# Rope stage of a decoder layer regrouped from pairs of heads to fours, with the rope weights as 32x64 tiles

## The chip, the cores and the metric

The kernel runs on one core of a Trainium2 chip. The metric is the device time of one execution in microseconds. Three runs before the change gave a median of 886.24 us (886.09 to 887.56).

## What is computed

One decoder layer over 32 sequences of 64 tokens, width 256, all in float32. Three blocks follow one another, each with a residual and a layer norm: linear attention, cross attention with rotary positions, and a mixture of 32 experts with the best 8. The change lies in the cross attention, and in what is computed between its parts. Cut to that (16 heads, R = 64, D_C = 64, D_CQ = 192, K = 128):

```python
q_hk = (hidden_q @ Wq.T).reshape(Bv, Sv, H, K)
q_big = jnp.einsum('bshk,hkq->bshq', q_hk, w_kc_q)
q_big = _apply_rope(q_big, sin_q[None, :, None, :], cos_q[None, :, None, :])
kv_r = _apply_rope(kv_c, sin_k[None], cos_k[None])
q_r = jnp.einsum('bshq,hqr->bhsr', q_big, W_qr)
k_r = jnp.einsum('bld,hdr->bhlr', kv_r, W_kr)
scores = jnp.einsum('bhsr,bhlr->bhsl', q_r, k_r)
attn = jax.nn.softmax(scores, axis=-1)
```

Rope multiplies each of the 192 rows of `q_big` by a cosine and adds its partner row, 96 rows away, times a sine.

## The kernel before

The tokens go in four blocks of 512. For each block a linear attention part, then `pairs` (the rope stage) and then `cross` (scores, softmax, context) run. The five engines have a program of their own each, written out by hand and joined by semaphores. `cross(b)` also holds the linear attention of block b + 1, so the order is `linear(0)`, `pairs(0)`, then `cross(b)` and `pairs(b + 1)` for b = 0 to 2, then `cross(3)` and the experts. Weights are folded once: `fold_a` multiplies Wq by w_kc_q for each head (`a_hi`, `a_lo`), `fold_m` multiplies W_qr by W_kr (`m_w`, 64 columns a head), so that a head's query goes straight to the 64 channels of the latent keys.

The rope stage handles 8 pairs of heads. For a pair, TensorE (PE) makes three chunks of 128 rows into three PSUM banks: 18 matmuls of 128x128 by 512 columns (`split_matmuls`, L245 to L247: a float32 product as three products of high and low parts). Chunk 0 has rows 0 to 63 of both heads, chunk 1 their partners 96 to 159, chunk 2 rows 64 to 95 and 160 to 191. VectorE (DVE) multiplies from PSUM with the tables `ropeq` (`times`, L1055): four products of chunks 0 and 1 into `prod`, two of chunk 2 straight into `roped`. GpSimd (POOL) adds the two pairs of products (L749). Chunk 2 is not added: its rows go into the next product twice, once with the cosine and once with the sine. `latent_q` (L1436) then multiplies four chunks of `roped` with `m_w`: 16 matmuls of 64x64 by 256 columns, each of which the profile shows as two records, so 32. They use the four quarters of the array, and stand on PE behind the 18 products of the following pair. ScalarE (ACT) copies the result to `lq` (L842).

PE waits at pair p for the DVE products of pair p - 2 (`s_rp`); two sets of three banks alternate. Banks 6 and 7 hold the result of `latent_q`, which waits for the ACT copy of the pair before (`s_lq`). Between the rope products DVE also runs, for the block before, the norm of its last 128 tokens (`norm2`, behind pair 0) and its expert routing (`shift_logits` behind pair 2, six parts of `route` behind pairs 3 to 5), and for the next block the root mean square norm (`rms`, behind pair 5). Within each of these, a small instruction waits for the one before it.

At the end of the stage PE runs `latent_q(6)` and `latent_q(7)`, turns the next block's x (`turn_x`), computes `scores(0)`, and DVE starts the softmax (`shift`, L1100) while PE runs projections.

## Time and profile before

| | |
|---|---|
| median of 3 runs | 886.24 us |
| the profiled execution | 886.25 us, of which the span is 884.4 |
| PE busy | 851.1 us |
| DVE busy | 634.8 us |
| ACT, POOL busy | 277.7, 144.9 us |
| granted clock of PE | 0.995 of full speed |
| rope stage of block 0 | from 53.3 us |
| rope stages of blocks 1 to 3 | from 159.9, 268.5 and 377.6 us |
| experts | from 460.8 us |

Busy time is the time in which at least one instruction of the engine runs. Matmuls overlap, so the spacing of their starts tells more than their duration. Line numbers are those of the kernel.

### The profile page before, as it was taken

To read this page: it belongs to the slowest core of one execution; us is meant where nothing else is said; L and a number is where in the kernel's file an instruction comes from. 1 tells how busy PE (TensorE), PEld (TensorE's weight loads), DVE (VectorE), ACT (ScalarE), POOL (GpSimd) and SP (SyncE) were. 2 spreads that over 40 slices of the span, in tenths; PEclk is the share of its full clock that TensorE was granted. 3 is DMA by queue.
4 is the path that set the end of the run, shared out by engine and by line. 5 is a ranking of instruction groups with operands and counts; after the bars stand their busy time and mean duration, and the time that the engine had idled before them with its cause. 6 is when DMAs were issued, how large, how long until landed. Compare 5 with 4: busy or idle time off the path is not lost.

```text
span 884.4 us, 14757 instructions
## 1 busy us (share of the span) xinstructions
PE 851.1 (96%) x5742; PEld 671.2 (76%) x5742; DVE 634.8 (72%) x1383; ACT 277.7 (31%) x498; POOL 144.9 (16%) x123
## 2 busy tenths in 40 slices
PE   8999999999999989999899999999999999999995
PEld 6967677676777767777578778888888888887884
DVE  5566787878878888788677776766575666666587
ACT  4431243112422124220353522433323333232242
POOL 2024301333013330133340400300000000000120
PEclk9999999999999999999999999999999999999998
DMA  9210000100001000000230014110212020000011
GB/s 345 115 37 1 1 2 1 49 1 18 1 1 49 1 17 1 0 25 4 81 109 1 25 32 150 44 59 1 90 48 66 0 85 29 35 1 1 1 47 49
DMA packets 12830, 35.84 MB, mean 41 GB/s; under 512 B 1504, under 2 KB 2400, under 8 KB 12256
## 3 DMA queue, kind: packets, MB, share of 16 engines
q1 hardware_dynamic: 12768, 34.98, 11.5%
q8 instruction: 42, 0.69, 0.4%
q14 instruction: 20, 0.16, 0.1%
HBM read 30.33 MB, written 2.36 MB: 37 GB/s over the span
## 4 chain that ended last, share of the span: by engine, by line
PE 85%; DVE 9%; issue 3%; ACT 2%; DMA 0%; POOL 0%; ACTq 0%; DVEq 0%
PE ps L245 21%; PE ps L246 20%; PE ps L247 20%; PE ps L1436 7%; PE ps L1516 5%; PE ps L1507 3%; PE ps L1308 2%; PE ps L1492 1%; PE ps L1345 1%; PE ps L1483 1%; DVE xT_lo L968 1%; PE ps L1375 1%; PE ps L1301 1%; PE ps L1291 1%; PE ps L1262 1%
## 5 line engine op out<-in xcount | busy, mean ns | idle before, releaser
L518 DVE TENSOR_TENSOR su<-sg,ps 128x512 f32<-128x512 f32 x96 | 66.0, 687 | 121.4 <-PE ps L247 118.2
L245 PE MATMUL ps<-y_hi,f_hi 128*128 128x512 f32 x384 | 151.2, 394 | 1.3 <-issue 1.3
L247 PE MATMUL ps<-y_hi,f_lo 128*128 128x512 f32 x384 | 149.5, 389 | 0.0
L246 PE MATMUL ps<-y_lo,f_hi 128*128 128x512 f32 x384 | 149.4, 389 | 0.0
L376 ACT ACTIVATE sg<-ps 128x512 f32<-128x512 f32 x96 | 57.4, 599 | 250.6 <-PE ps L247 250.6
L749 POOL TENSOR_TENSOR roped<-prod 128x512 f32<-128x512 f32 x64 | 80.9, 1286 | 169.9 <-DVE prod L1055 169.9
L1055 DVE TENSOR_TENSOR prod<-ps,ropeq 128x512 f32<-128x512 f32 x128 | 79.3, 681 | 27.2 <-PE ps L247 27.0
L245 PEld LDWEIGHTS ps<-y_hi,f_hi 128*128 128x128 f32 x384 | 72.1, 188 | 16.9 <-issue 2.2
L247 PEld LDWEIGHTS ps<-y_hi,f_lo 128*128 128x128 f32 x384 | 72.1, 188 | 15.2
L246 PEld LDWEIGHTS ps<-y_lo,f_hi 128*128 128x128 f32 x384 | 72.1, 188 | 15.1 <-issue 0.5
L245 PE MATMUL ps<-xT_hi,a_hi 128*128 128x512 f32 x192 | 78.4, 408 | 3.7 <-DVE xT_lo L968 3.7
L245 PE MATMUL ps<-h_hi,f_hi 128*128 128x512 f32 x192 | 75.4, 393 | 1.4 <-DVE h_lo L349 1.4
L524 DVE TENSOR_TENSOR hc<-su,cb 128x512 f32<-128x512 f32 x96 | 72.0, 750 | 6.0
L246 PE MATMUL ps<-xT_lo,a_hi 128*128 128x512 f32 x192 | 75.4, 393 | 0.0
L247 PE MATMUL ps<-xT_hi,a_lo 128*128 128x512 f32 x192 | 74.9, 390 | 0.0
L247 PE MATMUL ps<-h_hi,f_lo 128*128 128x512 f32 x192 | 74.8, 389 | 0.0
L246 PE MATMUL ps<-h_lo,f_hi 128*128 128x512 f32 x192 | 74.8, 389 | 0.0
L842 ACT ACTIVATE lq<-ps 128x512 f32<-128x512 f32 x28 | 16.8, 599 | 159.0 <-PE ps L1436 159.0
L1436 PE MATMUL ps<-roped,m_w 64*64 64x256 f32 x1024 | 63.1, 383 | 2.9 <-ACT lq L842 2.9
L349 DVE TENSOR_TENSOR h_lo<-hc,h_hi 128x512 fp32r<-128x512 f32 x88 | 62.6, 712 | 0.1
L370 ACT ACTIVATE h_hi<-hc 128x512 fp32r<-128x512 f32 x96 | 59.9, 624 | 3.4 <-DVE hc L524 3.4
L1516 PE MATMUL ps<-u_w,roped 128*128 128x256 f32 x256 | 58.2, 380 | 2.1 <-ACT roped L874 2.1
(161 smaller groups left out, 1336.9 us busy)
## 6 DMA issues: line engine op xcount, KB each, us to landing
cb<-routing SPq DMA_DIRECT2D x32, 256.0 KB
f_raw<-in_L_ffn_gate_up_proj SPq DMA_DIRECT2D x8, 768.0 KB, 6.2
f_raw<-in_L_ffn_down_proj SPq DMA_DIRECT2D x8, 384.0 KB, 7.0
xb<-in_x SPq DMA_DIRECT2D x4, 512.0 KB, 4.2
lq<-in_L_xattn_Wq SPq DMA_DIRECT2D x1, 2048.0 KB, 14.7
x2T_all<-in_L_xattn_Wo SPq DMA_DIRECT2D x1, 2048.0 KB, 12.0
x2T_all<-x2T SPq DMA_DIRECT2D x4, 512.0 KB, 3.3
roped<-in_L_xattn_w_kc_q SPq DMA_DIRECT2D x1, 1536.0 KB, 10.0
```

What stands on the lines that cost most here:

```text
L245: pe.matmul(dst, l_hi, r_hi, start=first, stop=False, skip_group_check=check)
L246: pe.matmul(dst, l_hi, r_lo, start=False, stop=False, skip_group_check=check)
L247: return pe.matmul(dst, l_lo, r_hi, start=False, stop=last, skip_group_check=check)
L349: eng.tensor_tensor(h_lo[:, k % 3], hc[:, k % 2], h_hi[:, k % 3].bitcast(F32), ALU.subtract).then_inc(s_hlo, 1)
L370: act.activation(h_hi[:, k % 3], hc[:, k % 2], ACT.Copy).then_inc(s_hhi, 1)
L376: act.activation(sg[:, k % 2], bank(2 * (k % 2)), ACT.Silu).then_inc(s_sg, 1)
L518: dve.tensor_tensor(su[:, k % 2], sg[:, k % 2], bank(2 * (k % 2) + 1), ALU.mult).then_inc(s_su, 1)
L524: dve.tensor_tensor(hc[:, k % 2], su[:, k % 2], cb[:, w, cols(n)], ALU.mult).then_inc(s_hc, 1)
L749: pool.tensor_tensor(roped[:, p % 2, k], prod[:, 2 * k], prod[:, 2 * k + 1], ALU.add)\
L1055: return dve.tensor_tensor(t64(dst), t64(bank(src)), ropeq[:, table, :].unsqueeze(1).broadcast_to((P, SEQS, SEQ)), ALU.mult)
L1436: mm = pe.matmul(ps[r:r + 64, q_bank(p, h), 0:256], m_w[i, p, k * DC:(k + 1) * DC], roped[i, p % 2, k, 256 * th:256 * th + 256], start=k = ...
L1516: mm = pe.matmul(ps[:, f, 0:D], ct[:, c, :], u_w[:, (c + 4 * (t // 2)) % 8, :], start=c == 0, stop=c == PAIRS - 1)
```

## The change

The rope stage works on four heads (a quad: pairs 2g and 2g + 1, j = 0 or 1) and makes six chunks for them, each with 32 rows of each head. Chunks 0 and 1, 2 and 3, 4 and 5 are partners. A step for two partner chunks is called a slot; 12 slots make a block, with 12 matmuls of 512 columns each. Slots use banks 0, 1 and 2, 3 in turn; PE waits at slot t for the DVE products of slot t - 2. DVE makes four products a slot into three buffers in turn (`made`), POOL adds both pairs, and a ring of four slots holds the sums. No row goes into `latent_q` twice. `latent_q(g, c)` has 16 matmuls of 32x64 by 256 columns for each slot, on the eight 32x64 parts of the array; each of the four row parts writes to a bank of its own (banks 4 to 7). The three of a quad stand together, behind slots 4, 7 and 10; those of the last quad behind slot 11, with `turn_x` and the scores of six pairs moved ahead of the last one.

On DVE the norm, the routing and the root mean square norm are cut into single steps. After each product `side` issues the steps due there: `norm2` in slots 0 and 1, `shift_logits` behind slot 3, 22 routing steps from the third product of slot 4 to the end of slot 9, 12 steps of the root mean square norm in slots 6 to 8. The arithmetic of these steps is as before. ACT has its other work (`x1` copy, squares, exp) ahead of its `lq` copies. `fold_m` writes 32 columns at a time, in 24 matmuls for two pairs in place of 16. The order and tables of the inputs follow the new rows. Left out below: `route_step` and `rms_step` with the old instructions one by one, and the host's reordering.

```diff
+QUADS = PAIRS // 2
+SLOTS = 3 * QUADS
...
-    a_hi = sb(att, "a_hi", [P, KC, PAIRS, 3 * P], F32R)
-    a_lo = sb(att, "a_lo", [P, KC, PAIRS, 3 * P], F32R)
-    m_w = sb(att, "m_w", [P, PAIRS, 4 * DC])
-    ropeq = sb(att, "ropeq", [P, 6, SEQ])
+    a_hi = sb(att, "a_hi", [P, KC, QUADS, 6 * P], F32R)
+    a_lo = sb(att, "a_lo", [P, KC, QUADS, 6 * P], F32R)
+    m_w = sb(att, "m_w", [P, QUADS, 6 * DC])
+    ropeq = sb(att, "ropeq", [P, 12, SEQ])
...
-    roped = sb(att, "roped", [P, 2, 4, BT])
+    roped = sb(att, "roped", [P, 8, BT])
...
+    prod2 = sb(att, "prod2", [P, 2, BT])
...
-    LOGITS = ps[:, 5, 0:TILES * EXPERTS]
+    LOGITS = ps[:, 7, 0:TILES * EXPERTS]
     m_bank = lambda g, h: 4 + (g + h) % 2
-    q_bank = lambda p, h: (6 if p < PAIRS - 1 else 2, 7)[h]
+    lq_bank = lambda b, g, j: 0 if g == QUADS - 1 and j == 1 and b < BLOCKS - 1 else 4 + 2 * j
+    score_bank = lambda b: 2 if b < BLOCKS - 1 else 0
+    turn_bank = lambda b: 2 - score_bank(b)
+    made = lambda i: (prod[:, 0:2], prod[:, 2:4], prod2[:, 0:2])[i % 3]
+    a_pair = lambda a, k: a[:, k % KC, k // KC // 2].rearrange("p (r h j c) -> p r h j c", h=2, j=2, c=32)[:, :, :, k // KC % 2]
+    a_psum = lambda k: ps[:, k % 4, 0:384].rearrange("p (r h c) -> p r h c", h=2, c=32)
...
-    C_BANKS = (6, 7, 5, 4)
+    C_BANKS = (2, 3, 6, 4)
...
-            for p in range(PAIRS):
+            for t in range(SLOTS):
                 for k in range(2):
-                    pool.wait_ge(s_rp, 24 * b + 3 * p + k + 1)
-                    if p >= 2 and k == 0:
-                        pool.wait_ge(s_qr, 8 * b + p - 1)
-                    pool.tensor_tensor(roped[:, p % 2, k], prod[:, 2 * k], prod[:, 2 * k + 1], ALU.add)\
+                    pool.wait_ge(s_rp, 24 * b + 2 * t + k + 1)
+                    if t >= 4 and k == 0:
+                        pool.wait_ge(s_qr, SLOTS * b + t - 3)
+                    pool.tensor_tensor(roped[:, 2 * (t % 4) + k], made(2 * t + k)[:, 0], made(2 * t + k)[:, 1], ALU.add)\
                         .then_inc(s_rope, 1)
...
+        def lq_out(b, p):
+            f = lq_bank(b, p // 2, p % 2)
+            act.wait_ge(s_qr, SLOTS * b + 3 * (p // 2) + 3)
+            act.activation(lq[:, p].rearrange("p (h n) -> p h n", h=2), ps[:, f:f + 2, 0:256], ACT.Copy)\
+                .then_inc(s_lq, 1)
+
         def pairs(b, later, following):
             act.wait_ge(s_x1, 4 * b + 4)
             if later:
                 x2T_out(b - 1, 2, 5)
-            else:
-                act.activation(x1[:], xn[:], ACT.Copy).then_inc(s_x1c, 1)
-            for p in range(PAIRS):
-                act.wait_ge(s_qr, 8 * b + p + 1)
-                if p < PAIRS - 1:
-                    act.activation(lq[:, p].rearrange("p (h n) -> p h n", h=2), ps[:, 6:8, 0:256], ACT.Copy)\
-                        .then_inc(s_lq, 1)
-                else:
-                    act.activation(lq[:, p, 0:256], ps[:, q_bank(p, 0), 0:256], ACT.Copy)
-                    act.activation(lq[:, p, 256:512], ps[:, q_bank(p, 1), 0:256], ACT.Copy).then_inc(s_lq, 1)
-                if later and p == 0:
-                    x2T_out(b - 1, 3, 2)
-                    act.activation(x1[:], xn[:], ACT.Copy).then_inc(s_x1c, 1)
-                if later and p == 2:
-                    act.wait_ge(s_lsub, b)
-                    act.activation(rt[:, 1], rt[:, 0], ACT.Exp).then_inc(s_lexp, 1)
-                if following and p == 1:
-                    act.wait_ge(s_x1c, b + 1)
-                    squares(b + 1)
+                x2T_out(b - 1, 3, 4)
+            act.activation(x1[:], xn[:], ACT.Copy).then_inc(s_x1c, 1)
+            if following:
+                act.wait_ge(s_x1c, b + 1)
+                squares(b + 1)
+            if later:
+                act.wait_ge(s_lsub, b)
+                act.activation(rt[:, 1], rt[:, 0], ACT.Exp).then_inc(s_lexp, 1)
+            for p in range(PAIRS - 2):
+                lq_out(b, p)
+            for m in range(2 if following else 0):
+                xT_hi_out(b + 1, m, s_xt, s_xthi)
+            lq_out(b, PAIRS - 2)
+            lq_out(b, PAIRS - 1)
...
+            def side(i):
+
+                if later and i + 1 < len(NORM2_PARTS):
+                    for j in range(NORM2_PARTS[i], NORM2_PARTS[i + 1]):
+                        norm2_step(b - 1, 3, j)
+                if later and i == 4 * 3 + 3:
+                    shift_logits(b - 1, LOGITS)
+                if later and 0 <= i - (4 * 4 + 2) < ROUTE_COUNT:
+                    route_step(b - 1, i - (4 * 4 + 2))
+                if following and 0 <= i - 4 * 6 < RMS_STEPS:
+                    rms_step(b + 1, i - 4 * 6)
+
             own.need()
-            for p in range(PAIRS):
-                if following and p == 6:
-                    rms(b + 1)
-                f = 3 * (p % 2)
-                for k in range(3):
-                    if k < 2:
-                        if p >= 1:
-                            dve.wait_ge(s_rope, 16 * b + 2 * p - 1 + k)
-                        dve.wait_ge(s_q, 24 * b + 3 * p + 2)
-                        times(prod[:, 2 * k], f + k, 2 * k)
-                        times(prod[:, 2 * k + 1], f + 1 - k, 2 * k + 1).then_inc(s_rp, 1)
-                    else:
-                        if p >= 2:
-                            dve.wait_ge(s_qr, 8 * b + p - 1)
-                        dve.wait_ge(s_q, 24 * b + 3 * p + 3)
-                        times(roped[:, p % 2, 2], f + 2, 4)
-                        times(roped[:, p % 2, 3], f + 2, 5).then_inc(s_rp, 1)
-                if later and p == 0:
-                    norm2(b - 1, 3)
-                if later and p == 2:
-                    shift_logits(b - 1, LOGITS)
-                if later and 3 <= p < 6:
-                    route(b - 1, 2 * p - 6)
-                    route(b - 1, 2 * p - 5)
+            for t in range(SLOTS):
+                f, table = 2 * (t % 2), 4 * (t % 3)
+                for k in range(2):
+                    if 2 * t + k >= 3:
+                        dve.wait_ge(s_rope, 24 * b + 2 * t + k - 2)
+                    dve.wait_ge(s_q, 24 * b + 2 * t + 2)
+                    times(made(2 * t + k)[:, 0], f + k, table + 2 * k)
+                    side(4 * t + 2 * k)
+                    times(made(2 * t + k)[:, 1], f + 1 - k, table + 2 * k + 1).then_inc(s_rp, 1)
+                    side(4 * t + 2 * k + 1)
...
+        NORM2_PARTS, RMS_STEPS, ROUTE_COUNT = (0, 1, 2, 4, 6, 8, 10, 11), 12, 22
...
-                for p in (2 * g, 2 * g + 1):
-                    for k in range(4):
+                for c in range(6):
+                    for j in range(2):
                         for h in range(2):
                             r = slice(64 * h, 64 * h + 64)
-                            o = (p % 2 * 4 + k) * DC
-                            mm = pe.matmul(ps[r, m_bank(g, h), o:o + DC], l_qr[r, p, k, :], r_kr[r, p, :],
+                            q = 64 * h + 32 * j
+                            mm = pe.matmul(ps[q:q + 32, m_bank(g, h), c * DC:(c + 1) * DC],
+                                           l_qr[r, 2 * g + j, 32 * c:32 * c + 32], r_kr[r, 2 * g + j, :],
...
+            def latent_q(g, c):
+
+                for k in range(2):
+                    pe.wait_ge(s_rope, 24 * b + 2 * (3 * g + c) + k + 1)
+                    w = slice((2 * c + k) * DC, (2 * c + k + 1) * DC)
+                    ring = 2 * ((3 * g + c) % 4) + k
+                    for th in range(2):
+                        for j in range(2):
+                            for h in range(2):
+                                i = slice(64 * h + 32 * j, 64 * h + 32 * j + 32)
+                                r = 64 * (h ^ th)
+                                mm = pe.matmul(ps[r:r + 64, lq_bank(b, g, j) + h, 0:256], m_w[i, g, w],
+                                               roped[i, ring, 256 * th:256 * th + 256],
+                                               start=c + k == 0, stop=c + k == 3)
+                mm.then_inc(s_qr, 1)
...
+            for t in range(SLOTS):
+                g, c = t // 3, t % 3
+                if t == 1:
                     pe.wait_ge(s_bdT, 2 * b + 2)
+                if t >= 2:
+                    pe.wait_ge(s_rp, 24 * b + 2 * t - 2)
+                for k in range(2):
+                    a = slice((2 * c + k) * P, (2 * c + k + 1) * P)
+                    for kc in range(KC):
+                        mm = split_matmuls(pe, bank(2 * (t % 2) + k), a_hi[:, kc, g, a], a_lo[:, kc, g, a],
+                                           xT_hi[:, kc, :], xT_lo[:, kc, :], kc == 0, kc == KC - 1)
+                    mm.then_inc(s_q, 1)
+                if later and t == 0:
                     pe.wait_ge(s_bdT, 2 * b + 2)
                     turn_x2(b - 1, 2, 5)
+                if later and t == 2:
                     pe.wait_ge(s_r2, 4 * b)
                     pe.wait_ge(s_ct, 8 * b)
+                    turn_x2(b - 1, 3, 4)
+                if later and t == 3:
                     logits(b - 1, LOGITS)
+                if t in (4, 7, 10):
+                    g = t // 3 - 1
+                    if g >= 1:
+                        pe.wait_ge(s_lq, 8 * b + 2 * g)
+                    if later and g == 0:
                         pe.wait_ge(s_lsub, b)
+                    for c in range(3):
+                        latent_q(g, c)
+            pe.wait_ge(s_lq, 8 * b + PAIRS - 2)
+            pe.wait_ge(s_rp, 24 * b + 22)
+            latent_q(QUADS - 1, 0)
+            latent_q(QUADS - 1, 1)
+            for m in range(2 if following else 0):
+                turn_x(n, m, s_xn, s_xt)
+            if following:
+                pe.wait_ge(s_rp, 24 * b + 24)
+            scores(b, 0, 0, PAIRS - 2)
+            latent_q(QUADS - 1, 2)
...
-                pe.wait_ge(s_lq, 8 * b + 7)
-                turn_x(n, 0, s_xn, s_xt)
-                pe.wait_ge(s_lq, 8 * b + 8)
-                turn_x(n, 1, s_xn, s_xt)
-                scores(0)
                 projection(n, 0)
+                scores(b, 0, PAIRS - 2)
                 projection(n, 1)
-                scores(1)
+                scores(b, 1)
...
-                pe.wait_ge(s_lq, 8 * b + 7)
+                pe.wait_ge(s_rp, 24 * b + 24)
                 turn_c(pe, 0)
-                pe.wait_ge(s_lq, 8 * b + 8)
                 turn_c(pe, 1)
-                pe.wait_ge(s_rp, 24 * b + 24)
+                scores(b, 0, PAIRS - 2)
                 turn_c(pe, 2)
-                scores(0)
-                keep_warm(6, 3)
-                scores(1)
+                keep_warm(6, 7)
+                pe.wait_ge(s_cT, 2)
+                scores(b, 1)
```

## Rows read from the trace of the kernel before

**Rows 1.** The page's chain that ended last, by engine, share of the span.

```profile
PE 85%; DVE 9%; issue 3%; ACT 2%; DMA 0%; POOL 0%; ACTq 0%; DVEq 0%
```

**Rows 2.** Busy time by stretch, rope stage of block 1: stretch, length, PE, PEld, DVE, ACT, POOL.

```profile
159.86:207.70 47.84, 47.84 (x356) 35.37 (x356) 41.29 (x123) 7.09 (x19) 17.74 (x14) 1.00 0.09 30
```

**Rows 3.** Groups of instructions in 159.7 to 208 us: count, busy us, mean ns.

```profile
L1055 DVE TENSOR_TENSOR prod<-ps,ropeq 128x512 f32<-128x512 f32 x30 | 18.6, 681 | 3.0 <-PE ps L247 3.0
L749 POOL TENSOR_TENSOR roped<-prod 128x512 f32<-128x512 f32 x14 | 17.7, 1290 | 35.4 <-DVE prod L1055 35.4
```

**Rows 4.** Timeline of one pair, block 0: start us, length us, then the instruction.

```profile
67.96 1.96 PE L1436 MATMUL ps<-roped,m_w 64*64 64x256 f32 x32
69.84 0.50 PE L245 MATMUL ps<-xT_hi,a_hi 128*128 128x512 f32 x1
70.19 0.40 PE L246 MATMUL ps<-xT_lo,a_hi 128*128 128x512 f32 x1
...
72.51 0.39 PE L247 MATMUL ps<-xT_hi,a_lo 128*128 128x512 f32 x1
...
73.01 0.69 DVE L1055 TENSOR_TENSOR prod<-ps,ropeq 128x512 f32<-128x512 f32 x1 [2.56 <-PE ps L247]
...
73.87 0.39 PE L247 MATMUL ps<-xT_hi,a_lo 128*128 128x512 f32 x1
74.19 0.45 PE L1436 MATMUL ps<-roped,m_w 64*64 64x256 f32 x4
```

**Rows 5.** L1436 in stretches of 0.02 us; in brackets the records running.

```profile
67.96:67.98 0.02, 0.02 (x4) 0.02 (x4) 1.00 0.00 0
...
68.44:68.46 0.02, 0.02 (x7) 0.02 (x3) 1.00 0.00 0
```

**Rows 6.** The chain in order of time: start us, length us, what.

```profile
17.09 2.08 PE ps L1331 x64
...
117.86 1.09 PE ps L1483 x64
...
121.45 3.46 PE ps L1516 x16
```

**Rows 7.** Timeline of DVE in block 1, routing steps and products.

```profile
186.57 0.47 DVE L1157 MAX8 top<-rt 128x8 f32<-128x32 f32 x4
187.08 0.09 DVE L1160 MATCH_VALUE_LOAD rt<-top,rt 128x8 f32 x1
...
187.25 0.08 DVE L1160 MATCH_VALUE_LOAD rt<-top,rt 128x8 f32 x1
...
187.85 0.29 DVE L1162 SCALAR_TENSOR_TENSOR rt<-rt 128x128 f32<-128x128 f32 x1
188.06 2.48 DVE L1055 TENSOR_TENSOR prod<-ps,ropeq 128x512 f32<-128x512 f32 x4
...
192.09 0.17 DVE L1169 TENSOR_SCALAR rs<-rs 128x4 f32<-128x4 f32 x1
192.17 0.22 DVE L1170 SCALAR_TENSOR_TENSOR rs<-top,rs 128x4 f32<-128x4 f32 x1
```

**Rows 8.** Timeline, end of block 1's rope stage, PE and DVE.

```profile
207.48 0.39 PE L247 MATMUL ps<-xT_hi,a_lo 128*128 128x512 f32 x1
...
210.47 2.20 PE L1436 MATMUL ps<-roped,m_w 64*64 64x256 f32 x32 [0.72 <-ACT lq L842]
...
215.38 0.68 DVE L1100 TENSOR_REDUCE small<-ps 128x8 f32<-128x512 f32 x1
```

**Rows 9.** Timeline, end of block 3's rope stage, PE and DVE.

```profile
425.32 0.39 PE L247 MATMUL ps<-xT_hi,a_lo 128*128 128x512 f32 x1
...
433.28 0.69 DVE L1100 TENSOR_REDUCE small<-ps 128x8 f32<-128x512 f32 x1 [5.15 <-issue]
```

**Rows 10.** Timeline behind `fold_m`, weight load of PE's next product.

```profile
19.10 0.19 PEld L245 LDWEIGHTS ps<-xT_hi,w_hi 128*128 128x128 f32 x1
```

**Rows 11.** Timeline of DVE at the start of block 1's rope stage, last of `norm2`.

```profile
162.51 0.41 DVE L954 TENSOR_SCALAR x<-x,small 128x256 f32<-128x256 f32 x1
```

227 lines of the change are left out of this document (116 added, 111 removed).

## The prediction, made before the changed kernel ran

> **What bounds the kernel now.** I read the chain that ended last first: 85% of it is PE [rows 1]. Then the stretches: in the rope stage of block 1 PE is busy all of its 47.84 us, but DVE is busy 41.29 of them [rows 2], and of its idle time 3.0 us is a wait for PE's products [rows 3]. So this stage is PE's, with DVE close behind. The timeline of a pair gives its period: `latent_q` starts at 67.96 and again at 74.19, 6.23 us later [rows 4]. Inside, from the second to the eighteenth product (70.19 to 73.87) there are 16 spacings of 0.230 us [rows 4]; the first takes 0.35 (69.84 to 70.19), 0.12 more, as every start behind another kind of work does. 18 x 0.230 = 4.14, which leaves 2.09 us of a pair for `latent_q`. Its 32 records start in sets of four: four run at 67.96, and seven or eight near each new start [rows 5]. A full-array product with 256 columns takes 3.46 / 16 = 0.216 us a record [rows 6]. Eight sets at 0.216 are 1.73 us; the other 0.36 us of the 2.09 is the price of going from full-array work to tiles and back.
>
> **What the change removes on PE.** The products with `a_hi` and `a_lo` stay 144 a block. `latent_q` had 8 x 32 = 256 records a block and gets 12 x 32 = 384, but if eight tiles run at once there are 48 sets in place of 64. No row before shows eight tiles at once. The lower bound of a set is the stream of one tile, 0.216 us, which a full array and four tiles share. The upper bound is two sets of four behind each other, 0.432. Between them: 64 records of 64 columns take 2.08 us where two tiles work (L1331) and 1.09 where four do (L1483) [rows 6], so a set of two takes 0.065 and a set of four 0.068; twice the tiles cost 0.003 us a set, and one record went out every 0.017 us, 0.136 for eight, under 0.216. I take 0.216.
>
> The Trainium skill, "TensorEngine Tiling (Array Packing)", Key Properties, says that different tiles run loads and matmuls in parallel and lists 32x64 as eight tiles; the trace bears this out for four 64x64 tiles and shows nothing on eight. By it the sum stays as it is. "TensorE: Matmul & The Clock Gate", Part 3, gives about 4 ns for each further tile of a set; the four tiles here show no such surplus per set (four tiles and the full array both take 0.216), and as an estimate from that page four more tiles on 192 sets would take back 3 us.
>
> Before the last product of a block stood six bursts of 2.09, 12.5 us. Now three stand there, of 12 sets each: 3 x (2.59 + 0.36) = 8.9. That is 3.7 us less a block, 14.7 in four, if nothing waits.
>
> **What waits instead.** The slots are the new point. PE takes 12 x 0.230 = 2.76 us for one, and slot t may not start before DVE has finished slot t - 2, because two pairs of banks alternate. DVE starts 0.27 us behind the last of the products (72.51 + 0.23 to 73.01) [rows 4], its products start every 0.60 (four in 2.48 with a last one of 0.68), and the last ends 0.69 on: 0.27 + 1.80 + 0.69 = 2.76. With 0.05 for the signal (my estimate) it is 2.81 against 2.76, and PE's restart costs 0.12. So wherever two slots follow each other with no burst between, PE loses 0.16, before any small step. Before, a set of three banks had 6.23 us between its reuses against some 3.8 of DVE, and this could not happen.
>
> The small steps that now stand between two products of a slot lengthen it. Their price, when the product hides their latency, is the start spacing: 0.21 for a 128x128 step (187.85 to 188.06), 0.08 for a tiny one (192.09 to 192.17), 0.66 for four match-and-replace (four times 187.08 to 187.25), 0.42 for four MAX8 [rows 7]. Below, they could cost nothing; above, their price was the spacing with the wait for each other, some 1.4 times that (0.77 us from 187.08 to 187.85, 0.51 from 186.57 to 187.08). By place:
>
> - Slots 2, 4, 7 and 10 of block 0 have only the 0.16 each, and slot 10 0.27 more from three tiny steps: 0.9 us.
> - Start of blocks 1 to 3: the turn of x2 now stands behind slot 0, 2.76 us into the stage, and wants `norm2(2)`, which ended at 162.92, 3.06 us in [rows 11]: 0.35. Then the `norm2(3)` steps in slots 0 and 1 (some 0.6 and 0.8 us) make slots 2 and 3 wait 0.25 and 0.5. Together 1.1.
> - Slot 7: slot 5 has the routing steps with MAX8 and match-and-replace between its products: 0.21 + 0.42 + 0.66 = 1.29, so 0.16 + 1.29 = 1.45.
> - Slot 10: slot 8 has three tiny steps (0.27) and three routing steps (0.7): 0.16 + 0.97 = 1.13, without the tiny ones 0.86 in block 3.
> - The turns and the logits no longer stand beside a burst, so two restarts of 0.12 come in: 0.2.
>
> Sum of the waits: 0.9 in block 0, 3.9 in blocks 1 and 2, 3.6 in block 3. Against 3.7: +2.8, -0.2, -0.2, +0.1, so 2.5 us faster in all. In the later blocks the waits take the whole gain of the tiles.
>
> POOL has 24 additions of some 1.27 us a block for 16 [rows 3], 31 us of 48, one for each 1.2 us of products in a slot; it lags up to 1.4 us behind DVE. `latent_q` runs a slot and more later, so this is hidden; without that cover it would cost up to 1.4 us a burst. The ring of four slots is free in time, since the burst behind slot 4 frees slot 0 before POOL reaches slot 4.
>
> **Behind the last product.** In block 1 the softmax starts on DVE 7.67 us after it (207.71 to 215.38) [rows 8]; 0.72 of that was `latent_q(7)` waiting for the ACT copy, which goes. Two bursts (4.2) become one of two slots and one of a single slot, 2.1 + 1.2 = 3.3. But `projection(n, 0)`, 6 x 0.230 + 0.12 = 1.5, now stands before the scores of the last pairs: 7.67 - 0.72 - 0.9 + 1.5 = 7.55. 0.1 for each of three blocks. From there to the first turn of weights DVE's own chain decides, unchanged. PE then has one projection and not two to cover the softmax's start; that wait falls where PE would have waited anyway. In block 3 (7.73 before [rows 9]) no projection comes in, but the last `latent_q` waits for POOL's last sum, 0.27 + 1.80 + 0.69 + 0.07 + 1.29 = 4.1 behind the last product; then 0.5 for it, 1.2 for two ACT copies and 0.6 for the scores, with 0.3 of handshakes: 6.7. Of the 1.0 I take 0.7, because ACT now has the third `cT` copy ahead of the exponentials. Together 1.0.
>
> **The folds.** `fold_m` writes with four 64x32 tiles at once and not two 64x64: 48 records for 64, in sets of four at 0.068. Its second half takes 0.8 for 2.08 [rows 6], and the next product stood at its end, 19.10 [rows 10]. Bounds 0 and 2.5; DVE's copies of `m_w` come between, so I take 0.6. `fold_a` has the same records and copies of the same size in another order: nothing. The first load is smaller and is not waited for. `route` in the experts part has the same steps: nothing.
>
> **Sum.** 2.5 + 1.0 + 0.6 = 4.1. The profiled execution took 886.25, the median 886.24, so I forecast 882.1.
>
> **Rivals.**
>
> - Eight tiles do not run at once. From a set of 0.216 + 4.1 / 192 = 0.237 on the change no longer gains; at 0.432 it costs 192 x 0.216 = 41 us, less some 4 us of DVE waits that this hides: 919. For it: nothing in the trace has more than four at once, and four banks are written at a time for two. Against: two to four tiles cost 0.003. A set between 0.237 and 0.3 gives 886 to 898. Chance 0.08 for the full price, 0.10 for between.
> - DVE is not late. If small steps vanish behind products, the waits fall to 0.9 or less a block and the sum is 4 x 2.8 + 1.6 = 12.8: 873; without handshakes at all 870. For it: DVE's busy time sees its chains shortened. Against: 41.29 of 47.84 busy. Chance 0.17.
> - DVE is later than I think. At 1.4 times the step price blocks 1 to 3 lose 1.5 us more each: 887, no change or slightly slower. Chance 0.12.
> - The forecast, 878 to 886, around 882.1: 0.53.
>
> The range 868 to 891 takes in the second, third and last and the lower part of the first: 0.8 of the chance or a little more. A measurement here tells about 0.2% (1.8 us) from no change. Faster: 0.40 of the 0.53 and the 0.17, 0.59 with a little of the rest. Within 0.2%: 0.16. Slower: 0.25.
>
> **What would show it.** In the profile after: `latent_q` bursts of about 2.6 us for 96 records, with eight records starting within 0.05 us and sets 0.216 apart (if they are 0.43, the first rival). PE's waits for DVE's products before slots 7 and 10, near 1.4 and 1.1 us in blocks 1 to 3, under 0.5 in block 0. Block 0's rope stage near 43 us from first to last product for 45.7, the others' near 48. The prediction is wrong if block 1's stage is much shorter than 47 us (DVE was not late) or the bursts are longer than 3.1 us.

## The result, and the profile of the changed kernel

The changed kernel takes 906.6 us (median of 4 runs, 905.4 to 909.3), the kernel before 886.26 beside it (4 runs, 886.09 to 887.56): a ratio of 1.0234, 95% interval 1.0221 to 1.0246. It is 20.3 us slower; forecast were 882.1 us, in a range of 868 to 891. The profiled execution took 905.4 us, its span is 903.6.

First the stages, by the starts of the products with `a_hi` and `a_lo` (the end is the start of a block's last product plus 0.23; by these starts the stages of blocks 2 and 3 of the kernel before begin at 268.8 and 377.7 us). A crossing is the stretch from the end of one block's rope stage to the start of the next one's.

| stretch | before, us | after, us | difference | forecast |
|---|---|---|---|---|
| up to block 0's rope stage | 53.30 | 57.78 | +4.5 | -0.6 |
| rope stage of block 0 | 45.74 | 43.61 | -2.1 | -2.8 |
| of block 1 | 47.85 | 54.86 | +7.0 | +0.2 |
| of block 2 | 47.85 | 56.21 | +8.4 | +0.2 |
| of block 3 | 47.85 | 50.82 | +3.0 | -0.1 |
| three crossings (60.82, 61.08, 61.06 before) | 182.96 | 181.45 | -1.5 | -0.3 |
| behind block 3's last product | 458.9 | 458.9 | 0.0 | -0.7 |

The sum of the differences is the 19.2 us between the spans. So the loss has two places: the start, and the rope stages of blocks 1 to 3.

The timeline of TensorE (PE) in block 1 of the changed kernel, start us, length us, and in brackets its idle time and what ended it; the first burst of latents is with it:

```profile
165.09 0.41 PE L1425 MATMUL ps<-ident,x 128*128 128x128 f32 x2 [0.15 <-DVE x L960]
173.56 0.41 PE L1425 MATMUL ps<-ident,x 128*128 128x128 f32 x2 [2.26 <-DVE x L1149]
...
181.59 2.85 PE L1509 MATMUL ps<-roped,m_w 32*64 32x256 f32 x96
...
191.25 0.50 PE L254 MATMUL ps<-xT_hi,a_hi 128*128 128x512 f32 x1 [1.14 <-DVE prod L1058]
...
202.35 0.50 PE L254 MATMUL ps<-xT_hi,a_hi 128*128 128x512 f32 x1 [2.35 <-DVE prod L1058]
...
208.15 0.50 PE L254 MATMUL ps<-xT_hi,a_hi 128*128 128x512 f32 x1 [1.36 <-DVE prod L1058]
```

Two things are to be seen. The 96 records of 32x64 tiles take 2.85 us, with 0.216 x 12 = 2.59 expected and the tail of the last record on top; in the trace their starts come in sets of eight, 0.216 us apart, so eight tiles do run at once. And PE waits for VectorE (DVE) four times for 7.1 us in all, where before it waited for nothing [rows 2]. So DVE is what to read. Its timeline in the middle of slot 6, and below it GpSimd's (POOL's) in the same stretch:

```profile
193.43 0.16 DVE L1218 TENSOR_SCALAR rs<-rs 128x4 f32<-128x4 f32 x1
193.50 0.21 DVE L1219 SCALAR_TENSOR_TENSOR rs<-top,rs 128x4 f32<-128x4 f32 x1
193.63 1.27 DVE L1163 TENSOR_SCALAR small<-small 128x4 int32<-128x4 int32 x1
194.82 0.68 DVE L1058 TENSOR_TENSOR prod<-ps,ropeq 128x512 f32<-128x512 f32 x1
...
196.36 0.27 DVE L1225 TENSOR_TENSOR rt<-rt,rs 128x128 f32<-128x128 f32 x1
196.56 1.28 DVE L1171 SCALAR_TENSOR_TENSOR small<-small 128x4 f32<-128x4 f32 x1
```

```profile
193.59 1.28 POOL L758 TENSOR_TENSOR roped<-prod 128x512 f32<-128x512 f32 x1 [1.03 <-DVE prod L1058]
196.51 1.30 POOL L758 TENSOR_TENSOR roped<-prod 128x512 f32<-128x512 f32 x1 [1.64 <-DVE prod L1058]
```

A step on four columns takes 1.27 or 1.28 us, and ends where POOL's addition ends: 193.63 + 1.27 = 194.90 beside 193.59 + 1.28 = 194.87, and 197.84 beside 197.81. The steps that began before the addition, L1218 and L1219 at 193.43 and 193.50 and L1225 at 196.36, took their usual 0.16, 0.21 and 0.27. So the step's own work is not what takes long: the one that meets a running addition is drawn out. The groups of DVE in block 1 (161 to 217 us; busy us, mean ns) say which forms are hit:

```profile
L1171 DVE SCALAR_TENSOR_TENSOR small<-small 128x4 f32<-128x4 f32 x3 | 2.7, 892 | 0.0
L1147 DVE SCALAR_TENSOR_TENSOR small<-small 128x1 f32<-128x1 f32 x3 | 2.6, 860 | 0.1
L1166 DVE TENSOR_SCALAR xn<-xb,small 128x256 f32<-128x256 f32 x4 | 2.2, 604 | 0.0
...
L1186 DVE TENSOR_REDUCE rs<-rt 128x4 f32<-128x128 f32 x5 | 1.4, 271 | 0.0
L1231 DVE TENSOR_SCALAR rt<-rt,alpha 128x128 f32<-128x128 f32 x1 | 1.3, 1324 | 0.0
L1163 DVE TENSOR_SCALAR small<-small 128x4 int32<-128x4 int32 x1 | 1.3, 1268 | 0.0
...
L1207 DVE MAX8 top<-rt 128x8 f32<-128x32 f32 x4 | 0.5, 176 | 0.0
```

In the kernel before the same steps, in helper lines, take 0.16 (L1171), 0.16 (L1147), 0.35 (L1166), 0.28 (L1231) and 0.17 us (L1163). Counted over 57 to 450 us, with at least 0.15 us of a POOL instruction left when the step starts: all 25 steps with two tensors from SBUF are drawn out to its end (within 0.16 us), and so are all 12 `tensor_scalar` steps from SBUF to SBUF on 4, 128 or 256 columns. Not hit are `tensor_scalar` steps on one column (9 of 9 keep their 0.14 to 0.15 us with 0.64 to 0.89 us of an addition left), reductions, reciprocals, MAX8, match-and-replace, and whatever reads one operand from PSUM, the big products (0.65 to 0.69 us) among it. The Trainium skill, "SBUF — State Buffer", section "Who interferes with whom", has this rule: VectorE and GpSimd share a pair of ports, held by whichever instruction starts first until it ends, and VectorE needs it for a second SBUF input or in a two-port mode. The list above agrees with it for the steps with two inputs; which `tensor_scalar` steps run in such a mode no trace shows, only that those on one column are not held. Below, the lock stands for this waiting of one engine's instruction for the other's end.

In all, DVE is busy 47.78 us of block 1's stage, and 39.00 in the experiment below in which the additions are short.

Last the start. TensorE's timeline through `fold_m`:

```profile
14.72 1.54 PE L1390 MATMUL ps<-x2T_all 64*32 64x64 f32 x96
16.89 1.33 PE L1390 MATMUL ps<-x2T_all 64*32 64x64 f32 x81 [0.62 <-ACT m_w L826]
21.72 0.42 PE L1390 MATMUL ps<-x2T_all 64*32 64x64 f32 x15 [3.50 <-issue]
22.07 0.50 PE L254 MATMUL ps<-xT_hi,w_hi 128*128 128x512 f32 x1
```

Behind the 177th record, 15 before its end, PE stands still for 3.50 us, released by nothing that the profile shows; before, the next product began at 19.10 [rows 10], now at 22.07. From 22.96 to 25.52 the products start 0.43 us apart for 0.23, and the granted clock of 22 to 27 us is 0.66, so that TensorE ran at the lower of its two levels (1.2 GHz) in a part of it. That is the other 1.5 us of the start's 4.5.

### The profile page after: what moved, and what is told of

The parts are those of the page before. It is cut to its first block and busy times, and to the rows that moved or that the text cites. A ratio compares the mean times of both kernels' runs of the same rounds, so it can differ in the third digit from the quotient of the medians.

```text
span 903.6 us, 15942 instructions
## 1 busy us (share of the span) xinstructions
PE 845.1 (94%) x6318; PEld 671.6 (74%) x6318; DVE 652.1 (72%) x1383; ACT 275.9 (31%) x494; POOL 186.7 (21%) x155
## 5 line engine op out<-in xcount | busy, mean ns | idle before, releaser
L758 POOL TENSOR_TENSOR roped<-prod 128x512 f32<-128x512 f32 x96 | 122.7, 1289 | 154.6 <-DVE prod L1058 153.9
L1058 DVE TENSOR_TENSOR prod<-ps,ropeq 128x512 f32<-128x512 f32 x192 | 124.4, 679 | 34.4 <-PE ps L256 33.6
L254 PE MATMUL ps<-xT_hi,a_hi 128*128 128x512 f32 x192 | 81.5, 424 | 16.5 <-DVE prod L1058 12.5
L256 PE MATMUL ps<-xT_hi,a_lo 128*128 128x512 f32 x192 | 76.9, 400 | 0.0
L358 POOL TENSOR_TENSOR h_lo<-hc,h_hi 128x512 fp32r<-128x512 f32 x8 | 10.3, 1283 | 286.1 <-ACT h_hi L379 286.1
L254 PEld LDWEIGHTS ps<-xT_hi,a_hi 128*128 128x128 f32 x192 | 37.0, 193 | 36.2 <-DVE prod L1058 21.5
```

The source lines that it names most:

```text
L254: pe.matmul(dst, l_hi, r_hi, start=first, stop=False, skip_group_check=check)
L256: return pe.matmul(dst, l_lo, r_hi, start=False, stop=last, skip_group_check=check)
L358: eng.tensor_tensor(h_lo[:, k % 3], hc[:, k % 2], h_hi[:, k % 3].bitcast(F32), ALU.subtract).then_inc(s_hlo, 1)
L758: pool.tensor_tensor(roped[:, 2 * (t % 4) + k], made(2 * t + k)[:, 0], made(2 * t + k)[:, 1], ALU.add)\
L1058: return dve.tensor_tensor(t64(dst), t64(bank(src)), ropeq[:, table, :].unsqueeze(1).broadcast_to((P, SEQS, SEQ)), ALU.mult)
```

## The experiments

Fifteen kernels ran. The theories of the rope stages are **A**: a DVE step that meets POOL's addition is held to its end; **B**: the steps' own number and length is what costs; **C**: the lateness of products and latents, whoever makes it. Those of the start are **D**: PE's instructions arrive too slowly in `fold_m`, behind the weight loads; **E**: it is the form of the fold.

**Additions cut short.**

```diff
-pool.tensor_tensor(roped[:, 2 * (t % 4) + k], made(2 * t + k)[:, 0], made(2 * t + k)[:, 1], ALU.add)
+pool.tensor_tensor(roped[:, 2 * (t % 4) + k, 0:16], made(...)[:, 0, 0:16], made(...)[:, 1, 0:16], ALU.add)
```

> The changed kernel with GpSimd's additions cut from 512 columns to 16 (so 496 of 512 columns of the rotated queries are left out; every instruction and wait stays). Theory A, the port: VectorE's small steps with two SBUF operands wait for GpSimd's addition of 1.29 us to end. With additions of about 0.1 us their mean falls back from 0.4 to 1.3 us to about 0.2, and the rope stages of blocks 1 to 3 fall from 54.9, 56.2 and 50.8 us to 46 to 49, that of block 0 stays near 43.6; the kernel ends at 883 to 892 instead of 906.6. Rival B, the steps themselves or the turns between VectorE, TensorE and the queues that they make late: the stages stay above 52, the kernel above 900.

Measured in one execution, in which 496 of 512 columns of the sums are left out: 885.71 us, rope stages 42.92, 48.11, 48.16 and 47.87. In its groups of DVE and POOL (57 to 480 and 57 to 430 us):

```profile
L1171 DVE SCALAR_TENSOR_TENSOR small<-small 128x4 f32<-128x4 f32 x9 | 1.5, 172 | 0.0
...
L1147 DVE SCALAR_TENSOR_TENSOR small<-small 128x1 f32<-128x1 f32 x9 | 1.4, 160 | 0.3
```

```profile
L758 POOL TENSOR_TENSOR roped<-prod 128x16 f32<-128x16 f32 x96 | 21.5, 224 | 231.5 <-DVE prod L1058 225.5 <-PE ps L1509 6.0
```

Every step stands where it stood, and these take 0.17 and 0.16 us again, for 0.89 and 0.86 in block 1 above. B falls: of the time, 19.7 us between the two profiled executions hang on the length of POOL's instruction, 18.4 of them in the rope stages. This run can't tell the lock from POOL's lateness (C); the next two bear on that.

**The same trouble put into the kernel before.** Its step groups move from behind chunk 2's products, where POOL has nothing to add, to behind those of k = 1, where it starts to.

```diff
                         times(prod[:, 2 * k + 1], f + 1 - k, 2 * k + 1).then_inc(s_rp, 1)
+                        if k == 1:
+                            steps(p)      # norm2, shift, route from behind k == 2; rms from ahead of pair 6
```

> The kernel before, with its norm, shift, routing and rms groups moved from behind chunk 2's products to behind the products of k = 1, where GpSimd's addition of the same k is just starting; nothing else moves. Theory A: one step in each group that has two SBUF operands is drawn out to about 1.2 us (the others of the group run free once both additions are done), six groups a block, part of it on the path: 3 to 15 us slower than before (889 to 901). Rival B (no lock; the steps only need their own time): the records keep their 0.15 to 0.2 us and the time is within 2 us of before.

Measured: 901.55 us, ratio 1.0171 (1.0154 to 1.0188). In block 1's timeline of DVE one step of a group is long and the rest is not:

```profile
193.73 0.15 DVE L1171 TENSOR_SCALAR rs<-small 128x1 f32<-128x1 f32 x1
193.91 1.09 DVE L1173 TENSOR_SCALAR rs<-rs 128x4 f32<-128x4 f32 x1
...
201.16 1.23 DVE L1192 TENSOR_SCALAR rs<-rs 128x4 f32<-128x4 f32 x1
...
208.14 1.22 DVE L253 TENSOR_SCALAR small<-small 128x4 int32<-128x4 int32 x1
209.39 0.16 DVE L259 TENSOR_TENSOR small<-small 128x4 f32<-128x4 f32 x1
```

L1171 on one column keeps its 0.15 us although an addition has 1.25 us left; the next step, on four columns, is caught. This is the old kernel, with none of the new tiles, slots or banks, so the lock does not need them. The 15 us come from where the steps stand, but not all of them from the lock alone: the rope stages of blocks 1 to 3 grow by 1.7 each, 5.1 in all, and the crossings by 1.4 to 4.8. There the late groups (rms above all, which now comes four products later) also make the last `latent_q` late, with waits of 1.55 and 1.54 us behind block 1, and the granted clock of that crossing falls to 0.95. What each part is worth this run does not separate.

**POOL waits for the steps.**

```diff
+                    pool.wait_ge(s_steps, 24 * b + 2 * t + k + 1)   # POOL, ahead of each addition
+                if own.n > n:                                       # DVE, behind the steps of an odd place
+                    own.need()
+                dve.sem_inc(s_steps, 1)
```

> The changed kernel with the same steps at odd places only (behind a pair's second product), and GpSimd's addition of that pair waiting until the steps of its place are done. Nothing gets shorter, GpSimd starts later. Theory A: the steps run at 0.15 to 0.3 us each and the rope stages of blocks 1 to 3 fall to 47 to 50 us; the kernel takes 887 to 893. Rival C (what costs is latents and bank turns coming late, whoever makes them late): a later GpSimd makes the roped chunks later still, the stages stay above 54, the kernel at 905 or more.

Measured: 897.91 us, ratio 1.0133 (1.0116 to 1.0150); rope stages 43.46, 52.01, 51.79 and 50.15. The steps are short again (L1178, L1180 and L1182, the tiny steps of rms, some 0.15 us each), but for one: in each of three blocks one of the four `xn` steps (L1175) still takes 1.39 us for 0.34, under a POOL instruction with 1.24 us left. C expected 905 or more from a later POOL and is wrong; but A's number was missed by 5 us. Beside that step, two things that I added explain a part: rms now began in slot 3 and waited 2.24 us for ScalarE's squares, and places with steps cost DVE a handshake of 0.21.

**Groups in place of single steps, without and with POOL's wait.**

```diff
-                if later and 0 <= i - (4 * 4 + 2) < ROUTE_COUNT:
-                    route_step(b - 1, i - (4 * 4 + 2))
+                if later and i in (19, 25, 31):          # the same places with and without the wait
+                    route(b - 1, ...)                     # two parts each; norm2 whole at i == 3, rms at 37
```

> The changed kernel with the steps drawn together into groups (norm2 whole behind slot 0's last product, routing in three groups behind slots 4, 6 and 7, rms in one behind slot 9), GpSimd not held back. Theory A: a group loses one addition's time once, since GpSimd then finds no products to add and stays idle for the rest of the group; so five or six losses of 1 to 1.2 us a block in place of about ten: rope stages of blocks 1 to 3 at 50 to 53, the kernel at 892 to 900. A rival in which the whole cost is the number and length of the steps, which are the same: 905 or more.

> The same groups, and GpSimd's addition of the pair in front of each group waits until the group is done. Theory A: no step is drawn out, the rope stages of blocks 1 to 3 take 47.5 to 49.5 us, the kernel 885.5 to 890 (the start's 4.5 us are still lost). If GpSimd's lateness costs as much as the lock did: 50 to 53 and 892 to 900, as without the wait.

Measured: 900.32 us (1.0157, 1.0143 to 1.0172) without, rope stages 52.18, 52.08, 51.01; 894.21 (1.0086, 1.0072 to 1.0101) with, rope stages 49.84, 49.89, 48.78. Undoing the interleaving alone gives back 6 us, POOL's wait another 6. With it the crossings behind blocks 1 and 2 grew from 60.5 to 62.8, which I had not expected (below); this is the profiled execution, at 898.0 us the slowest of five, and it also begins block 0's stage at 58.66, 0.9 later than the changed kernel.

**The start.** First the fold alone, moved behind projection 5 with its copies on ScalarE and DVE, then (below) in halves behind 3 and 5.

```diff
-            fold_m()
             pe.wait_ge(s_wlo, 4)
-            for i in range(2, 8):
+            for i in range(2, 6):
                 projection(b, i)
+            fold_m()
```

> The changed kernel with fold_m and its two copies moved behind projection 5 on all three engines, nothing else. Theory D, TensorE idles 3.5 us inside fold_m because the fold's many short instructions are used up faster than their code arrives while the weight loads fill the DMA queues: later, with less DMA traffic, the idle time is gone and block 0's rope stage starts 4 to 5 us earlier (near 53.3), 902 us in all. Rival E, the fold's 32-column tiles cost this by themselves wherever they stand: idle time of 3 to 4 us moves with the fold, and the time stays within 1 us of 906.6.

Measured: block 0's rope stage starts at 54.10 for 57.78, idle time in the fold 1.06 us for 3.50. The total is 906.12, nearly unchanged (1.0227, 1.0209 to 1.0244): in the profiled execution the rope stages took 1.6 us more and what lies behind block 3's last product 1.3. Why, beyond that the rope stages shift with which step meets which addition, is not shown. So E is weakened and D is not shown by this run alone.

```diff
+        sp.wait_ge(s_mps, PAIRS // 2)
         load_kv(0)
         sp.dma_start(raw_kcq, a["L0_xattn_w_kc_q"]).then_inc(s_raw1, 16)
```

> The changed kernel with the sync engine's loads behind W_kr (context, w_kc_q, Wq, w_kc_kv and so on) held back until fold_m is through, so that the DMA engines are mostly idle while it runs. Theory D, TensorE's code arrives late behind the weights: the idle time of 3.50 us in fold_m falls to under 0.5, while the folds behind it may now wait for their weights. Rival E, that many short matmuls in a row stop for a reason of their own: 3 to 4 us of idle time as before.

Measured in one execution: 910.16 us, since `fold_a` now waits 4.98 us for Wq; but in `fold_m`:

```profile
17.02 1.33 PE L1391 MATMUL ps<-x2T_all 64*32 64x64 f32 x81 [0.62 <-ACT m_w L827]
18.84 0.42 PE L1391 MATMUL ps<-x2T_all 64*32 64x64 f32 x15 [0.49 <-issue]
```

The stop is behind the same record, the 177th, and lasts 0.49 us with idle DMA engines (a mean busy share of 0.01 in 12 to 17 us, for 1.00 in the changed kernel) where it lasted 3.50 with full ones. Nothing in `fold_m` waits for or reads what these loads bring. What comes over the same engines is the code: in the changed kernel the queue named "instruction" moved 0.03 MB in 12 to 27 us, two packets of 16 KB, against 5.74 MB of weights. So the stop's length is set by the loads; what PE waits for, the packets show further down.

```diff
+                    for k in range(4):
+                        mm = pe.matmul(ps[r, m_bank(g, h), o:o + DC], l_qr[r, p, 3, :], r_kr[r, p, :], start=True, stop=True)
```

> The kernel before with 32 more matmuls in fold_m (repeats of its last block, so 96 as in the changed kernel; the folded weights are right still). Theory D, instructions run out behind the weight loads: TensorE shows idle time of 1 to 4 us released by nothing in or behind fold_m and block 0's rope stage starts 2 to 5 us later than 53.3. Rival E, the form of the 64x32 tiles: no idle time, the extra 32 matmuls cost 1.0 us at 0.03 each, the stage starts near 54.3.

Measured in one execution: the stage starts at 57.07 for 53.30 in the kernel before, but with 0.17 us of idle time. D's idle time was missed, and E's start. The 32 added matmuls all lie in one row half, one tile at a time, and took 3.8 us in all, 0.12 each, so PE used its code up far more slowly than in the changed kernel; the later start is theirs. But the stop is again behind the 177th of 192 records, here of 64x64 tiles: its place does not hang on the form, and E falls.

The traces hold the instruction packets with their times, and these settle D further than the lengths do. Times in us; the packet is the first of 16 KB on the instruction queue:

| kernel | fold starts | record before the stop | stop starts | packet starts | PE goes on | behind the packet's start |
|---|---|---|---|---|---|---|
| changed | 14.72 | 177 | 18.22 | 19.17 | 21.72 | 2.55 |
| loads held back | 14.86 | 177 | 18.35 | 16.32 | 18.84 | 2.52 |
| before, more matmuls | 14.88 | 177 | 21.86 | 19.70 | 22.03 | 2.33 |
| fold behind projection 5 | 21.13 | 141 | 24.15 | 22.77 | 25.21 | 2.44 |
| fold in halves (below) | 17.85 | 141 | 23.25 | 21.46 | 23.88 | 2.42 |

In all fifteen kernels whose fold has 192 records, whatever the idle time, PE goes on 2.33 to 2.55 us behind the start of this packet. The stop has a fixed place in the program: 36 records earlier when 48 more products stand ahead of it. Against the changed kernel, holding back the loads brought the packet 2.99 us earlier, counted from the fold's start, and PE's restart 3.02. With PE slower to arrive there (21.86 for 18.22), nearly nothing of the stop is left. That is D. Which engine's code the packet carries no trace says; that PE waits for it rests on these times.

**Both causes together.**

```diff
+            fold_m(0, 2)                # behind projection 3
+            fold_m(2, 4)                # behind projection 5; the groups and POOL's waits as above
```

> The same again, with fold_m in two halves, behind projections 3 and 5, and its copies with it. Both causes together: the start is 3.5 to 4.5 us earlier than in the changed kernel (block 0's rope stage from 53.3 to 54.2), the kernel at 881.5 to 886, so faster than before by up to half a per cent. If either cause is not the one, 888 or more.

Measured: 889.36 us (1.0038, 1.0023 to 1.0052). The start is 52.77, 5.0 us earlier; the rope stages are as with the groups and POOL's wait, 43.98, 49.82, 49.93 and 48.76, and all three crossings take 62.8 in the profiled execution, which at 894.4 us is one of the two slowest. The eleven runs spread from 887.5 us at a granted clock of 0.994 to 894.6 at 0.985. The head of the first crossing shows why:

```profile
106.62 1.16 PE L1522 MATMUL ps<-bdT,lq 64*64 64x64 f32 x64 [1.30 <-DVE prod L1130]
108.18 0.72 PE L1594 MATMUL ps<-ident,prod 128*128 128x128 f32 x4 [0.40 <-DVE prod L1142]
109.74 1.11 PE L1594 MATMUL ps<-ident,prod 128*128 128x128 f32 x4 [0.83 <-DVE prod L1142]
110.50 0.78 PE L255 MATMUL ps<-xT_hi,w_hi 128*128 128x512 f32 x1
```

Behind these waits PE's products are 0.63 us long until 115.65; the granted clock is 0.74 in 104.75 to 112.75 and 0.83 in the 8 us behind. The kernel with groups and no split fold has the same three waits (1.30, 0.39 and 0.90) in its first crossing, with 0.66 for the turns, full clock and 60.49 us. So the half clock costs 2.3 us a crossing.

**Where the groups stand.**

```diff
+                if later and i in (31, 43): ...      # routing behind slots 7 and 10; norm2 in halves at 3 and 7
+                if following and i == 19: ...        # rms behind slot 4
```

> The last kernel with its groups put where VectorE waits for TensorE's latents: rms behind slot 4's last product, routing behind slots 7 and 10, norm2 in two halves behind slots 0 and 1; GpSimd waits for each group, for the multiplications of x too. By the trace VectorE idles 2.84 us at each burst of latents, which is where 3 us of steps should go: rope stages of blocks 1 to 3 at 46 to 48 instead of 49.8, the kernel at 877 to 885. If it is GpSimd's lateness that holds the stages at 49.8, nothing changes: 888 to 890.

> The same with nine matmuls on ones in front of the three waits of TensorE (1.30, 0.40 and 0.83 us) at the head of each crossing. In the kernel with split groups those waits were followed by 5 us at half clock in three crossings of three (62.8 us) and in another with the same waits in one of them by none (60.5). If the granted clock is what made 2.3 us of it, every crossing takes 60.5 to 60.8 here, and the kernel is up to 7 us faster than without (where those fall to half clock) and equal to it where they don't: 875 to 881.

> That kernel without GpSimd's waits for the groups: the same steps in the same places. Theory A: in each group one step is drawn out to the end of an addition of 1.29 us, five or six groups a block, some of it in time in which VectorE would idle: rope stages 1 to 3 us longer each in blocks 1 to 3, 3 to 8 us slower than with the waits. If GpSimd's waits do nothing but delay it: faster or equal.

Measured: 890.96 (1.0056, 1.0041 to 1.0071), 892.20 (1.0064, 1.0050 to 1.0078) with the matmuls on ones, and 902.66 (1.0190, 1.0175 to 1.0206) with them and without POOL's waits. The first two missed. In both, PE waits 1.99 to 2.00 us for x2 behind the halved norm2, and behind the last product of block 1 1.36 us for POOL, late from the group at slot 10. The crossings of blocks 1 and 2 take 62.7 and 62.3 with the ones and 62.1 and 61.7 without, the first 61.1 and 60.5. In the kernel without the ones the stages are 48.50, 50.02 and 48.11: better than 49.8 in two of three, and the rest is eaten up behind slot 10. The third is the cleanest number for the lock: same steps, same places, and 10.5 us more when POOL does not hold off, in the forecast direction and more than the 3 to 8 forecast. Its rope stages grow by 0.8, 2.3, 2.4 and 0.0 us; 2.2 more lie behind block 3's last product, where PE waits 1.75 us for POOL and then runs at half clock, and 2.1 of the 10.5 are not in the profiled executions. So POOL's waits are not only a delay: C is wrong here too.

**The last microseconds.** Two kernels with norm2 whole again, rms behind slot 4 and routing behind slots 6 and 9, one of them with six matmuls on ones; then one with that second group behind slot 8.

```diff
-                if later and i in (31, 43):
+                if later and i in (27, 39):      # the last kernel: (27, 35)
```

> Norm2 whole behind slot 0, rms behind slot 4, routing behind slots 6 and 9, so each a slot ahead of a burst of latents or right at it, GpSimd waiting for each. If GpSimd's lateness behind slot 10 was a cost, TensorE's waits for it behind the last products (1.36, 0.99 and 0.46 us) are gone, the rope stages of blocks 1 to 3 take 47.8 to 49, and the kernel 881 to 886 where the crossings keep their clock (60.5 us each), up to 7 us more where they don't. If the rest lies elsewhere: 888 or more with crossings of 60.5.

> The same with six matmuls on ones ahead of the waits at the head of each crossing (four ahead of the scores, two ahead of the turn's second half). If half the clock after those waits is the rest of the loss: crossings of 60.5 to 61.1 us in all three blocks, 882 to 885, and less scatter between runs than without. If it is not: the same time as without, or 1 to 2 us more for the added matmuls.

> The last groups kernel with its second routing group behind slot 8 instead of slot 9. GpSimd then catches up before the last burst: TensorE's wait of 1.1 us behind the last product is gone in blocks 1 to 3, the crossings of blocks 1 and 2 take 60.5 instead of 61.7, rope stages unchanged, so 3.3 us less: 882, faster than before by 0.4 per cent (0.9950 to 0.9965). If the wait was for something else: 885.4 again.

Measured: 885.37 (0.9996, 0.9987 to 1.0005), 886.45 (0.9999, 0.9990 to 1.0008) and 885.58 (0.9991, 0.9982 to 1.0000). The rope stages in the profile of the first are 43.05, 47.77, 48.02 and 47.79, no longer than with the additions cut short (42.92, 48.11, 48.16, 47.87). Its crossings of 61.7 had a wait of 1.14 for POOL's addition behind the group at slot 9. The last kernel lost that wait (crossings 60.49 three times), but PE then waits 0.54 more inside each stage and the stages take 48.6 to 48.9: of 3.3 us expected 1.0 came, in the profiled span (883.2 to 882.2), and none in the median. The ones bought nothing: 1.1 us more, within the scatter of both. The last kernel's runs again follow the clock: 884.0 and 884.2 us at 0.997, 887.5 at 0.990.

## Why the prediction was wrong

**Held.** Eight tiles at once: 2.85 us for a burst, the bounds of 0.216 and 0.432 a set were fair and the value was right. With the additions cut short block 0's stage takes 42.92 us, and 42.9 were forecast; in the changed kernel it takes 43.61, with one wait of 0.79 at slot 10 where 0.15 is seen with short additions, so the lock is in this block too: its rms steps for the next block are drawn out. The order behind the last product and its worth: crossings -0.33, -0.59 and -0.59 for -0.1 each, a little more than forecast; block 3's softmax starts 6.6 us behind the last product with 6.7 forecast, though the end of the kernel shows nothing of it. And the base of the argument, that in blocks 1 to 3 DVE takes back what the tiles give: with nothing held up, the stages are 48.1, 48.2 and 47.9 us (additions cut short) with 48.05, 48.05 and 47.75 forecast. The sums for these blocks were right for a kernel without the lock, and so were the places of the waits: 1.15 and 0.84 us before slots 7 and 10, where 1.45 and 1.13 were forecast with a restart of 0.12 in each.

**Failed: the price of a step.** "Above, their price was the spacing with the wait for each other, some 1.4 times that." This is the term that failed, and with it the waits built on it. The price of a step that meets an addition is what is left of the addition, up to 1.28 us, eight times the step's own 0.16. The rows for it came from steps that stood behind chunk 2's products, where POOL had done its additions (in 195.87 to 198.40, and the steps from 198.10 on); I took their duration along into a place where another engine was at work. The trace of the kernel before had the sign, outside the rope stage, in lines that I did not use:

```profile
151.84 2.62 POOL L733 TENSOR_TENSOR bd<-kv,kt 64x512 f32<-64x512 f32 x2 [47.31 <-PEq L1561]
```

```profile
153.37 1.11 DVE L259 TENSOR_TENSOR small<-small 128x4 f32<-128x4 f32 x1
...
154.90 0.16 DVE L259 TENSOR_TENSOR small<-small 128x4 f32<-128x4 f32 x1
```

The first L259 ends at 154.48 and POOL's second multiplication at 154.46; the same stands at 262.29 and 371.21.

In the same text stands that POOL "has 24 additions of some 1.27 us a block" and that its lateness is hidden: I asked when POOL would be late, and not whom it would make late. None of the rivals was this; "DVE is later than I think" had the right place and a quarter of the right price (1.5 us a block). The rope stages of blocks 1 to 3 grew by 18.3 us; with the additions cut short they grew by 0.6. Block 1 is 6.75 us longer than with short additions: 4.9 in PE's waits (7.36 for 2.46) and 1.84 in the spacing of its products. The longest wait, 2.35 before slot 9, stood in no term of the sum. Most of the second part is the clock: in 204 to 206 us, behind the wait of 2.35, the granted clock is 0.50. But it adds nothing of its own there. DVE is busy 20.54 of the 20.65 us from 187.50 to 208.15, and PE waits 1.36 for it behind the slow products; at full clock it would have waited the longer. In block 2 six products also run at half clock behind the wait of 2.24, from 289.4 on, where DVE in turn waits for PE; that block is 1.35 us longer than block 1.

**Failed: the folds.** 0.6 us were forecast with bounds of 0 and 2.5, and 4.5 were lost. The rate was right, the count was not: "48 records for 64" sets 24 matmuls beside 16, but as records (two a matmul) half the fold has 96 for 64. At 0.068 for a set of four that is 1.63 us and not 0.8; 1.54 were measured, for 2.08. So the two halves can give 1.1 us, less 0.4 more of waiting for the copies (0.62 for 0.21), and the bound of 2.5 was more than twice too high. That 0.6 is close to what is left is luck. The lower bound of 0 failed by the mechanism that the sum did not have: a gain of rate is only had if instructions come at that rate; 3.50 us of idle time and 1.5 of half clock behind it say that they did not, under full DMA queues. With the fold in halves further back the start is 52.8, 0.5 better than before, so that nearly the forecast 0.6 was there to be had.

**Together.** 906.6 is 24.5 over the forecast: 5.1 at the start (4.5 lost for 0.6 gained), 18.0 in blocks 1 to 3 and 0.7 in block 0; the crossings (1.2 less than forecast) and the end (0.7 more) nearly cancel, and 1.2 lie between the profiled execution and the median. With both causes removed and POOL made to wait the kernel comes to 885.4 and 885.6, even with the kernel before, not to 882.1: the waiting itself costs handshakes and pushes POOL's work back, and PE falls to half clock behind some waits (the mean granted clock of the last kernel's eleven runs is 0.990 to 0.997). The profiled execution of the last one, at a clock of 0.997, took 884.0. A layout of the steps in which DVE never needs two SBUF operands under an addition was not tried.

## What to carry to other kernels

A duration read from a trace holds for what ran beside it. Before small VectorE steps move, look at what GpSimd does at the new place: with two SBUF operands, or as `tensor_scalar` from SBUF to SBUF on four columns or more, a step of 0.16 us cost up to 1.28 here, and the record gives it away by ending with GpSimd's. Put such steps where GpSimd is idle, in groups (here some one addition's time lost a group), or let GpSimd start behind them. And when an edit makes many short instructions run faster, ask where the code comes from at that moment.

## What was not expected of the hardware

- Two small steps right behind a product still slip in ahead of the addition that the same product releases: 193.43 and 193.50 before 193.59. The third is caught.
- The same three waits of 1.30, 0.39 and 0.90 us left PE at full clock in one kernel (60.49 us for the crossing) and near-equal ones put it to half clock in another (62.83). Which one happens changes from run to run of one kernel: 887.5 us at 0.994, 894.6 at 0.985. Waits that come to the same sum don't cost the same.
- The 192 records of 64x32 tiles with 64 columns ran at 0.016 us each and stopped behind the 177th, for 0.49 us with idle DMA engines and 3.50 with busy ones; in the kernel before with more matmuls, 192 records of 64x64 tiles in some 8 us, the stop was behind the 177th too, and 0.17 long. One packet of 16 KB decides it.
- `tensor_scalar` on one column keeps its 0.15 us under an addition; on four columns it waits for the addition's end.
